# Thirteen identity products for TensorE in four waits of a four-layer model kernel

## The reference

```
x = act_qdq(x);  up = act_qdq(x @ Wup);  gate = act_qdq(x @ Wgate)
gate = act_qdq(gate * fixed_qdq_u16(sigmoid(gate)));  o = act_qdq(gate * up)
return o @ Wdown          # act_qdq: scale = max|x| / 32767, round, clip, times scale
```

## Time and profile before

| | us |
|---|---|
| median of 3 runs | 1411.71 |
| the three runs | 1417.38, 1410.06, 1411.71 |
| the profiled execution, its own time | 1414.87 |
| its span, first to last instruction | 1413.1 |
| TensorE matmul busy | 1240.8 (88%) |
| VectorE / ScalarE / GpSimd busy | 861.6 / 676.4 / 291.1 |
| mean granted TensorE clock | 0.966 |

### The profile page before, as it was taken

One profiled execution on the slowest core, in us unless ns is written; L12 is line 12 of the kernel. 1 busy time (PEld: TensorE's weight loads), 2 busy tenths in 40 slices (PEclk: granted clock), 3 DMA queues, 4 the chain that ended last, 5 costly groups with the idle time before them and its releaser, 6 DMA issues.

```text
span 1413.1 us, 26412 instructions
## 1 busy us (share of the span) xinstructions
PE 1240.8 (88%) x9301; PEld 962.8 (68%) x9301; DVE 861.6 (61%) x1828; ACT 676.4 (48%) x1358; POOL 291.1 (21%) x502
## 2 busy tenths in 40 slices
PE   4889970488999889999888999899999998898989
PEld 2455630156888889887777888498889754556877
DVE  3878668755456566656677565566554566664242
ACT  1556758545443334444444444244444375665553
POOL 1799400120002233330000013034310111100000
PEclk9999995699999999999999999999999999999999
DMA  8000010041050313104006001032020000000000
GB/s 310 1 2 2 2 75 0 32 169 61 1 202 26 108 45 101 48 25 178 28 1 266 37 7 48 25 107 75 29 90 2 1 2 1 1 1 1 0 15 16
DMA packets 42606, 75.71 MB, mean 54 GB/s; under 512 B 3816, under 2 KB 33520, under 8 KB 41584
## 3 DMA queue, kind: packets, MB, share of 16 engines
q1 hardware_dynamic: 38384, 65.62, 12.7%
q0 software_dynamic: 4096, 8.40, 1.9%
HBM read 59.72 MB, written 14.29 MB: 52 GB/s over the span
## 4 chain that ended last, share of the span: by engine, by line
PE 69%; DVE 15%; ACT 7%; issue 5%; POOL 2%; DVEq 1%; DMA 1%; SPq 0%; ACTq 0%; POOLq 0%
PE bank L1655 7%; PE bank L1644 7%; PE bank L1640 6%; PE bank L1699 5%; PE bank L1631 3%; PE bank L1433 3%; PE bank L1709 3%; PE bank L1499 3%; PE bank L1438 2%; PE bank L1440 2%; PE bank L1439 2%; PE bank L1624 2%; PE bank L1626 2%; PE bank L1625 2%; PE bank L1549 2%
## 5 line engine op out<-in xcount | busy, mean ns | idle before, releaser
L1892 ACT ACTIVATE SC<-bank 128x512 f32<-128x512 f32 x192 | 114.4, 596 | 217.9 <-PE bank L1640 123.2
L1979 DVE SCALAR_TENSOR_TENSOR SC<-bank,SM,SC 128x512 f32<-128x512 f32 x128 | 95.8, 749 | 124.9 <-PE bank L1644 108.2
L1655 PE MATMUL bank<-A,SC 128*128 x1024 | 136.9, 277 | 7.2 <-DVE SC L1979 6.2
L1644 PE MATMUL bank<-X,SC 128*128 128x128 f32 x1024 | 136.6, 276 | 6.1 <-DVE SC L2258 5.6
L1640 PE MATMUL bank<-X,SC 128*128 128x128 f32 x1024 | 135.6, 275 | 3.0 <-ACT SC L1876 2.8
L1640 PEld LDWEIGHTS bank<-X,SC 128*128 128x128 f32 x1024 | 126.2, 192 | 16.2 <-issue 10.2
L1655 PEld LDWEIGHTS bank<-A,SC 128*128 128x128 f32 x1024 | 125.5, 192 | 16.5 <-issue 15.6
L1644 PEld LDWEIGHTS bank<-X,SC 128*128 128x128 f32 x1024 | 124.5, 192 | 8.5 <-DVE SC L2258 8.4
L1699 PE MATMUL bank<-A 128*128 128x128 f32 x736 | 101.1, 281 | 11.1 <-DVE A L2408 5.6
L1792 ACT ACTIVATE A<-bank,SM 128x128 f32<-128x128 f32 x256 | 73.8, 383 | 66.2 <-DVE SM L2075 65.9
L1699 PEld LDWEIGHTS bank<-A 128*128 128x128 f32 x736 | 91.0, 195 | 15.7 <-ACT A L1917 8.7
(11 more groups left out here) (322 smaller groups left out, 2613.5 us busy)
## 6 DMA issues: line engine op xcount, KB each, us to landing
A<-in_moe SPq DMA_DIRECT2D x36, 768.0 KB, 10.3
A<-xs SPq DMA_DIRECT2D x20, 256.0 KB, 3.4
ys<-A SPq DMA_DIRECT2D x20, 256.0 KB, 2.5
BW<-in_l1f SPq DMA_DIRECT2D x2, 2048.0 KB, 7.4
BW<-in_l2f SPq DMA_DIRECT2D x1, 3456.0 KB, 12.2
BW<-in_l1c SPq DMA_DIRECT2D x1, 3072.0 KB, 17.6
BW<-in_l3f SPq DMA_DIRECT2D x1, 2816.0 KB, 9.4
A<-in_l1c SPq DMA_DIRECT2D x1, 2560.0 KB, 8.7
```

The source lines that it names most:

```text
L1644: m = e.matmul(at["pu"].ap[:, cut(q)], wx[:, cut(4 + q)], x, start=True, stop=True)
L1655: m = e.matmul(o, at["h"].ap[:, cut(q)], W[:, bass.ds(r + (1024 + 128 * q), 128)], start=k == 0 and q == 0, stop=k == 1 and q == 3)
L1892: e.activation(at["h"].ap, at["pg"].ap, ACT.Gelu_apprx_tanh).then_inc(at["gelu"][0], 1)
L1979: return e.scalar_tensor_tensor(out=o, in0=a, scalar=s, in1=b, op0=o1, op1=o2)
```

## The change

The change adds a step kind `keep_on`, with n matmuls of the identity with itself into one bank of RB: stationary operand `ident` (128x128, fp32), moving operand `ident` repeated four times (512 columns). Nothing reads the bank afterwards; it is given back when the last of the n has finished. The step waits for the bank, and, where `after` is given, for that signal.

It is put in four places: behind the scores of the second head group of the first chunk in the attention of layer 0 (3 products) and of layer 3 (2 products), behind the `cond2` products ahead of `f0_magic` (4 products), and behind `p3` of the piece `nms[7]` with a wait for that DVE maximum (4 products). These are 13 products, 26 matmul records.

```diff
+        def keep_on(n, *after):
+            at = step("keep_on", n=n, after=after, pb=RB.take())
+            at["mm"] = tick("keep_on")
+            RB.give(at["pb"], at["mm"])
...
                             elif (n, j) != (3, 3):
                                 make_kb(n + (j == 3), (j + 1) % 4)
+                            if (n, j, half) == (0, 0, 1):
+                                keep_on(3 if i == 0 else 2)
...
         mx, mu, mg, mg2, mo = sm(4), sm(12), sm(12), sm(12), sm(12)
+        keep_on(4)
         at = step("f0_magic")
...
                 at["t"] = sig["o"] = tick("f0_vec")
+                if (n, m) == nms[7]:
+                    keep_on(4, at["t"])
...
+                elif kind == "keep_on":
+                    over(at["pb"])
+                    for s in at["after"]:
+                        w.wait_ge(*s)
+                    for _ in range(at["n"]):
+                        m = e.matmul(v4(at["pb"].ap), ident, bc_mid(ident, 4), start=True, stop=True)
+                    m.then_inc(at["mm"][0], 1)
```

## The result

The changed kernel takes 1406.39 us (median of 9 runs, 1404.35 to 1409.03), the kernel before 1411.1 us (9 runs, 1409.23 to 1417.49). The ratio is 0.9961, with a 95% interval of 0.9944 to 0.9977: 4.7 us or 0.39% less. The forecast was 1405.6 us and 0.43%. The profiled execution took 1409.03 us, with a span of 1407.2 us, 5.8 us less than the one before.

A forecast was written before the change was run, and what follows sets the result against it. PE, busy 88% of the span, was taken to bound the kernel where it ran at half clock behind waits. From 1413.5 us, gains of 0, 2.8, 2.5 and 2.6 us gave 1405.6 us; 8-in-10 range 1401 to 1411.

The forecast's parts named there:

- First place: Attention of layer 0, 3 products: PE comes earlier but then waits longer for POOL's copy of k; gain 0.
- the wait before 74 us: Attention of layer 0: PE's wait for POOL there grows by some 3 us, the scores behind it start unchanged.
- Second place: Ahead of `f0_magic`, 4 products: the 5.6 us at half clock behind them go at full clock; gain 2.8 us.
- forecast's sign of 1.00 from 182 us on: Ahead of `f0_magic`: full clock from 182 us to the end of the 24 products, which take 20.6 us, not 23.6.
- PE does not rest for longer than 0.7 us: Ahead of `f0_magic`: four products end at 185.6 us, 0.7 us before due work, so the clock stays full.
- Rival C: Second and fourth place: products run at half clock in front of due work, with no gain; 1416.2 us, chance 0.04.
- Third place: Behind `p3` of piece 7, 4 products: `down` starts at full clock and takes 10.3 us, not 13.1; gain 2.5 us.
- If fed: First ffn's 12 `down` products: 10.3 us provided input keeps up; a group is fed every 1.8 us, used in 2.6.
- Fourth place: Attention of layer 3, 2 products: halves the 10.2 us at half clock behind the wait; gain 5.1 us when profiled.
- Half of 5.1 us: Attention of layer 3: executions before lose the 5.1 us about half the time, so 2.6 us gain on average.
- rival B: Shifted timing makes other short gaps drop the clock; 1411.2 us with one fall, 1408.2 without; chance 0.22.
- base of 1413.5 us: Whole kernel: mean of four executions before, from which the average gain of 7.9 us was subtracted.

The follow-up runs named there:

- second candidate: The first candidate with its layer 1 attention burst moved to the second chunk and one product in each of three more waits; ratio to the kernel before 0.9945, median 1408.82 us.
- run with four banks: The changed kernel with the last products of the first ffn writing to the ring of four banks, not two; ratio to the kernel before 0.9945.
- fourth place alone: The changed kernel with only the 2 products in the attention of layer 3 kept; ratio to the kernel before 0.9991.
- the first and the fourth place alone: Two kernels, each the changed kernel with one burst kept: 3 products in layer 0's attention (ratio to before 1.0005), or 2 in layer 3's (0.9991).
- first candidate: The changed kernel without its layer 0 attention burst, with four banks and bursts in four further waits in layers 0 and 1; ratio to the kernel before 0.9959.

## Why the prediction was right

**First place: 0, as forecast.** The scores behind the wait for POOL came no earlier (30.3 us behind the first ones, against 30.0), and waits for POOL took up the gain. It was not the wait before 74 us that grew by 3 us, as the forecast said (5.02 us against 4.75), but mainly a new one of 2.19 us before 63.52 us. The chain of waits had said so the earlier trace rows.

**Second place: forecast 2.8, measured 2.1 and 2.8.** The mechanism held. The 24 products take 20.8 us, as the forecast said. In the changed kernel's profile the clock fell at 181.6 us, under the last conditioning product, and stayed at half until 185.0, against the forecast's sign of 1.00 from 182 us on; four products took 4.7 us, and the 24 began at 187.15, 0.8 us after they could have. The step of the prediction that was too short is "PE does not rest for longer than 0.7 us": it looked only at the rest that the burst fills, and not at the two ahead of it, of 1.41 and 0.87 us. Rival C had been argued down by the shorter of these rests. That they made the clock fall is not shown: the changed kernel's profile on another chip has the same fall (at 181.8 us) behind the same rests, but six profiles of variants with the same two rests have none and give the full 2.8 us. What decides between the two outcomes stays open.

**Third place: forecast 2.5, measured 2.0.** The clock rose during the burst, 3.3 us after its start and not after some 5.5, and `down` ran at full clock throughout. In the second candidate it rose only after 5.9 us, the burst took 6.6 us and the stage 13.35 us in place of 13.17: about the 0.2 us of loss that the forecast had as its bound, in one execution. "If fed" was checked for the quantized input only. The bank was left out: PE waits for `down_x` of the first group. That term is 0.4 us, shown by the run with four banks.

**Fourth place: forecast 5.1 in this execution, measured 4.8; 2.6 on average.** The burst ended on time and the clock stayed. Half of 5.1 us was a guess about other executions. In the four profiles without these products the loss is 4.8, 4.7, 1.6 and 1.6 us, 3.2 on average; the times of the fourth place alone give 1.3 us (-0.3 to 2.7). A third outcome, 3.4 us at half clock in place of 10.2 or none, was not foreseen.

**The sum.** Places two to four gave 8.8 us between the two profiles, close to the 10.4 forecast for them, but the executions differ by 5.8 us, since dips in other places came and went (+2.6 us net). This is the outcome that rival B foresaw, at the gap that the prediction named, and it happened beside the forecast and not in its place. That the shift in time caused it, as rival B has it, is not shown: the changed kernel's other profile has no dip at that gap. That the time came within 0.8 us of the forecast is in part luck. The base of 1413.5 us was 2.4 us above the median of the nine executions before, 1411.1 us, and the gain of 7.9 us was 3.2 us above the 4.7 us measured (3.2 to 7.9 us by the interval); the two errors cancel but for 0.8 us.

**Open.** Whether moved dips cost the changed kernel something on average is not settled. From the last addition of the first ffn to layer 3 half clock lasted 6.8 us in the profile before and 13.7 us in the changed kernel's, but only 3.4 us in the changed kernel's other profile, and 6.8 and 0 us in the first and the fourth place alone, where nothing ahead of it was changed but the first place. So the 13.7 us belong to that execution and need not be the usual case. The stretch itself took 842.6 and 845.2 us in the first two profiles and 846.0 to 852.0 us on the slower chips. The parts measured alone give -0.33%, +0.05% and -0.09% for places two to four, and the whole -0.39% and -0.47%. These agree within their intervals but do not prove that each part adds up.

## What to carry to other kernels

Before you fill a wait to hold the clock, ask what the engine's own lateness would cost behind it: where the chain runs on another engine the gain is zero, and where PE is the limit it is half the stretch at 0.50. A burst may be somewhat shorter than the wait: one product did as well as two where it left a rest of 0.70 us, while a burst that left 2.77 us lost the clock again. Each product that does not fit costs its full time. Ask also when the burst can start: one that had to wait 2.04 us for its bank, in a wait of 2.63 us, was 2.1 us late even at full clock. A dip behind a short wait is an event of one execution, so price it over several profiles, and expect the dips in other places to differ between two profiles, of the same kernel too.

## What the runs showed of the hardware

- Transposes of an fp32 identity raised the clock from 0.50 to 1.00 by themselves after 49 us of rest. Four of them take 0.43 us, against 0.86 us for one product with 512 fp32 columns.
- The clock can fall when PE is at work again: it fell 0.5 us after PE had resumed at 181.07 us, and in the second candidate 0.7 us after the burst had begun at 487.99 us behind a rest of 2.04 us. It need not: the same burst behind the same rest kept it at 491.46 us in the first candidate.
- The same gap had several outcomes for the same code: in layer 3, behind 1.76 us of rest, half clock for 10.2 us (two profiles) or for 3.4 us (two), and behind the gap before 329.72 us, which is 2.81 to 2.82 us long in thirteen profiles, none (five), 3.4 us (six) or 6.8 us (two).
- In the ten profiles with the third place the clock rose 3.2 to 5.9 us after the start of the burst, behind a rest of 49 us.
